# Decoder layer: attention scores take two pairs of PSUM banks in turn, probabilities get eight places, and the units are put in another order

## The reference

```
x = layernorm(x + self_attention(x))        # 16 heads; keys and values from a latent of 64, queries from one of 128
x = layernorm(x + cross_attention(x, ctx))  # 16 heads of 16; keys = values = ctx; out @ W.T + b
x = layernorm(x + experts(x))               # 8 experts of 256 -> 1024 -> 256, the best 2 of each token, weighted

scores = where(causal, q @ k.T / sqrt(48), -inf); out = softmax(scores) @ v     # self: content 16 + rotary 32 per head
h = gelu(x @ W1[e] + b1[e]);  y = h @ W2[e] + b2[e];  out = sum over the two experts e of weight * y
```

## Time and profile before

| | us |
|---|---|
| median of 3 runs | 747.67 (745.39 to 748.39) |
| the profiled execution | 746.01 |
| its span in the trace | 744.2 |
| TensorE busy | 623.2 (84%) |
| VectorE busy | 514.3 (69%) |
| ScalarE busy | 399.4 (54%) |
| GpSimd busy | 286.7 (39%) |

### The profile page before, as it was taken

How to read it: one execution, slowest core, us unless ns; L and a number is a source line. 1 busy time by engine, 2 the same in 40 slices (tenths; PEclk the granted TensorE clock), 3 DMA queues, 4 the chain that set the end, 5 groups by cost and what they waited for, 6 DMA issues and landing times.

```text
span 744.2 us, 22691 instructions
## 1 busy us (share of the span) xinstructions
PE 623.2 (84%) x8063; PEld 453.2 (61%) x8064; DVE 514.3 (69%) x1106; ACT 399.4 (54%) x847; POOL 286.7 (39%) x245
## 2 busy tenths in 40 slices
PE   3778889889999999888867677689999999999940
PEld 2456656666766666555644445667777777777720
DVE  6898789777866777546667764677766666666635
ACT  4345766667576574575865556344444444444414
POOL 3988454324555441511111010332444444454422
PEclk9899999999999999999997799799999999999985
DMA  8426551140403203213243014311222232222326
GB/s 274 118 65 172 160 165 37 46 142 11 106 3 100 59 13 121 70 37 80 77 152 89 27 57 142 114 31 30 45 44 45 45 52 42 42 42 42 49 41 208
DMA packets 39839, 59.45 MB, mean 80 GB/s; under 512 B 6768, under 2 KB 27504, under 8 KB 39632
## 3 DMA queue, kind: packets, MB, share of 16 engines
q1 hardware_dynamic: 32272, 48.12, 21.9%
q0 software_dynamic: 7488, 10.23, 8.5%
HBM read 34.08 MB, written 11.67 MB: 61 GB/s over the span
## 4 chain that ended last, share of the span: by engine, by line
PE 55%; issue 14%; DVE 13%; DMA 7%; ACT 6%; SPq 3%; POOL 1%; ACTq 1%; DVEq 0%; POOLq 0%
PE bank L1670 7%; PE bank L1272 4%; PE bank L1298 4%; PE bank L1672 4%; PE exp_scores L1323 3%; PE bank L1660 3%; DVE mxc L1062 3%; PE bank L1251 2%; PE max_scores L1660 2%; ACT probs L725 2%; PE bank L1662 2%; PE max_scores L1662 2%; PE max_scores L1661 2%; PE bank L1661 2%; PE bank L1252 2%
## 5 line engine op out<-in xcount | busy, mean ns | idle before, releaser
L725 ACT ACTIVATE probs<-exp_scores 128x768 f32<-128x768 f32 (+1 forms) x128 | 117.5, 918 | 118.5 <-PE exp_scores L1329 56.2
L615 POOL DMA_INDIRECT acc_rows<-x,slot_row x39 | 65.0, 1666 | 131.6 <-DVE x L1178 128.6
L1670 PE MATMUL bank<-w_sb,wp 128*128 x312 | 109.9, 380 | 1.6 <-DVE wp L1165 1.6
L1062 DVE TENSOR_REDUCE mxc<-max_scores 128x4 f32<-128x1024 f32 x64 | 78.1, 1221 | 38.2 <-PE max_scores L1343 38.0
L1672 PE MATMUL bank<-w_sb,wp 128*128 x312 | 85.0, 273 | 0.0
L794 ACT ACTIVATE probs<-bank,b_sb 128x128 f32<-128x128 f32 x152 | 43.5, 370 | 66.2 <-PE bank L1662 66.2
L794 ACT ACTIVATE probs<-max_scores,b_sb 128x128 f32<-128x128 f32 x160 | 45.6, 369 | 60.8 <-PE max_scores L1662 60.7
L1027 DVE TENSOR_REDUCE mx<-max_scores 128x6 f32<-128x768 f32 x64 | 61.0, 952 | 23.9 <-PE max_scores L1311 23.3
L1163 DVE CAST wp<-probs 128x512 f16<-128x512 f32 x78 | 33.8, 433 | 62.2 <-ACT probs L794 61.9
L1272 PE MATMUL bank<-probs,w_sb 128*32 128x256 f32 x768 | 57.3, 402 | 9.4 <-ACT probs L725 7.8
L1660 PE MATMUL max_scores<-xT,w_sb 128*128 128x128 f16 x320 | 61.3, 223 | 2.4 <-DVE xT L1157 2.4
(11 more groups left out here) (263 smaller groups left out, 1730.2 us busy)
## 6 DMA issues: line engine op xcount, KB each, us to landing
w_sb<-w_sb SPq DMA_DIRECT2D x192, 64.0 KB, 2.1
wstage<-in_w_exp SPq DMA_DIRECT2D x16, 512.0 KB, 4.2
w_sb<-in_w_exp SPq DMA_DIRECT2D x8, 512.0 KB, 4.9
wp<-in_w_exp SPq DMA_DIRECT2D x8, 512.0 KB, 3.8
x_sb<-in_x_by_feature SPq DMA_DIRECT2D x8, 256.0 KB, 3.6
x_res<-in_x SPq DMA_DIRECT2D x8, 256.0 KB, 3.0
ctx_raw<-in_ctx SPq DMA_DIRECT2D x8, 256.0 KB, 3.1
x_rows<-x SPq DMA_DIRECT2D x8, 256.0 KB, 2.7
```

The source lines that it names most:

```text
L615: nc.gpsimd.indirect_dma_start(out=acc_rows[:, :], out_offset=bass.IndirectOffsetOnAxis(ap=slot_row[:, n:n + 1], axis=0), in_=yb[n % 2], i ...
L725: nc.scalar.activation(probs[:, 2 * (k % 2):2 * (k % 2) + 2, 0:cols], ps_e[:, :, 0:cols], ACT.Exp, scale=(SELF_SCALE, CROSS_SCALE)[a]).the ...
L1062: nc.vector.tensor_reduce(mxc[:, 2 * k:2 * k + 2, :], ps_m[:, :, :].rearrange("p h (a k) -> p h a k", a=2), axis=AX.X, op=ALU.max).then_in ...
L1670: mm(o[:, 0:2 * D], ah[:, u, f, :], weights(e, at, 2 * D), start=(f == 0), stop=(f == FC - 1), skip_group_check=True)
```

## The change

- The two pairs of banks become `ps_p[0]` and `ps_p[1]`. A string of 288 digits, `SCORE_PAIRS`, says for each `sm`, `cm`, `st`, `se` and `ce` in TensorE's order which pair it takes; nearly always it is the other one than the unit before took (six times the same). `pair_free` waits for the reader of whatever unit was last in that pair. A stack now takes the first bank of its pair.
- `probs` gets eight places: groups of four heads alternate between two halves. The scratch that GpSimd's dynamic transfers use for their descriptors is halved (8192 bytes of each partition), as `probs` grows by 8192.
- All five orders are rewritten. Where TensorE's old order mostly alternated exponential units and maxima (94 exponential units stood alone between maxima or stacks), the new one has only 18 such and many runs of two to eight of one kind. `ge.4` moves from among the last `cm.7` to behind `cs.6` in VectorE's order, that is from before to after the maxima of batch 7 are complete. `gf.4` and `gR.4` move ahead of `cw.7`, and `gg.4` ahead of `cr.7` on GpSimd.
- New units `ft.4`, `fh.4`, `fl.4` transpose and split the slots of tile 0 inside attention, `ft.4` just before the last `lg.7` on TensorE, `fl.4` just before `lg.7` on VectorE.
- Several uses of the other banks move: `rope0` to bank 2, the gate's slots and table to bank 3, `cross_out` to bank 0, `cross_norm` to banks 0 and 1, and the two transposed maxima change places.
- The last tile: TensorE starts its first four `down` when the first half is split, and VectorE weights tile 37 before it splits the second half of tile 38.

The core of the diff:

```diff
+def pairs_in_turn():
+
+    uses = [x for x in order(TENSOR_ORDER) if x[0] in ("self_max", "cross_max", "stack", "self_exp", "cross_exp")]
+    return {use: int(bit) for use, bit in zip(uses, SCORE_PAIRS.replace("\n", ""))}
...
-        ps_fin = [ps_x[2], bank[1]]
+        ps_slots = [ps_x[3][:, 0:2 * P], bank[1][:, T:T + 2 * P]]
+        ps_fin = [ps_x[3], bank[1]]
         ps_kv, ps_q = ps_x[1], ps_x[1]
-        ps_qk = [ps_x[i] for i in (3, 1)]
-        ps_max = [ps_x[i] for i in (2, 0)]
+        ps_qk = [ps_x[i] for i in (2, 1)]
+        ps_max = [ps_x[i] for i in (0, 2)]
         ps_o = [[ps_x[i] for i in (0, 2)], [ps_x[i] for i in (1, 0)]]
-        ps_tok = [[ps_x[i] for i in (2, 0)], [ps_x[i] for i in (2, 1)]]
+        ps_tok = [[ps_x[i] for i in (2, 0)], [ps_x[i] for i in (0, 1)]]
         ps_back = [ps_x[i] for i in (0, 1)]
-        ps_out = [ps_x[i] for i in (0, 1)]
-        ps_sh = [ps_m[:, i, :].bitcast(F16) for i in range(2)]
+        ps_out = [ps_x[i] for i in (0, 0)]
+        ps_first = ps_x[1]
...
+                    half = k // 2 % 2
                     if k % 2 == 0:
                         for i in range(2):
-                            if done["exp", i] // 2:
-                                act_e.wait_ge(pe_pv[i], done["exp", i] // 2)
+                            if done[half, i]:
+                                act_e.wait_ge(pe_pv[i], done[half, i])
                     cols = (3 * P, 2 * T)[a]
-                    nc.scalar.activation(probs[:, 2 * (k % 2):2 * (k % 2) + 2, 0:cols], ps_e[:, :, 0:cols], ACT.Exp,
+                    nc.scalar.activation(probs[:, 2 * (k % 4):2 * (k % 4) + 2, 0:cols], ps_p[pair[u, k, b]][:, :, 0:cols], ACT.Exp,
                                          scale=(SELF_SCALE, CROSS_SCALE)[a]).then_inc(a_p[a], 1)
-                    done["exp", a] += 1
+                    if k % 2:
+                        done[half, a] = b * (H // 4) + k // 2 + 1
...
-            tile(N_TILES - 1, 0, False)
+            split_hidden(N_TILES - 1, 0, 0)
             weigh(N_TILES - 2, 1, (N_TILES - 3) * 16)
+            split_hidden(N_TILES - 1, 0, 1)
             weigh(N_TILES - 1, 0, (N_TILES - 2) * 16)
...
-            def exps_free():
-
-                once(a_p[0], at["self_exp"])
-                once(a_p[1], at["cross_exp"])
-
-            def maxima_free():
-
-                once(v_max[0], at["self_max"])
-                once(v_max[1], at["cross_max"])
+            held = [None, None]
+
+            def slots_in(n, u, loaded, target):
+
+                pe.wait_ge(g_ld[u], loaded)
+                for c in range(DC):
+                    last = nc.tensor.transpose(target[:, c * P:(c + 1) * P], xg[u][:, c * P:(c + 1) * P], ident)
+                last.then_inc(pe_ft, 1)
+
+            def pair_free(i):
+
+                if held[i]:
+                    once(*held[i])
...
                 elif u == "self_exp":
-                    exps_free()
+                    pair_free(pair[u, k, b])
...
                     last.then_inc(pe_t[0], 1)
-                    at[u] = b * (H // 2) + k + 1
+                    held[pair[u, k, b]] = a_p[0], b * (H // 2) + k + 1
                 elif u == "cross_exp":
-                    exps_free()
+                    pair_free(pair[u, k, b])
...
-            pe.wait_ge(v_al, 2 * N)
-            for f in range(FC):
-                down(0, f, last_at)
+            for half in range(2):
+                pe.wait_ge(v_al, 2 * N - 1 + half)
+                for f in range(4 * half, 4 * half + 4):
+                    down(0, f, last_at)
...
-    nc = bacc.Bacc("TRN2", target_bir_lowering=False, num_devices=1)
+    nc = bacc.Bacc("TRN2", target_bir_lowering=False, num_devices=1, dynamic_dma_scratch_size=8192)
```

The orders from batch 7's last maxima on, before and after. TensorE:

```diff
-cv1.6 st0.7 st1.7 ce5.6 x2.5 cm0.7 gr.4 cv2.6 ce6.6 cm1.7 lg.5 cm2.7 cm3.7 ce7.6 st2.7 st3.7 cm4.7 cv3.6 gs0.4 cm5.7
-co.6 cm6.7 cb.6 cm7.7 gs1.4 cn.7 ce0.7 cw.6 ce1.7 cv0.7 ce2.7 ce3.7 gs2.4 cv1.7 ce4.7 ce5.7 cv2.7 ce6.7 x2.6 ce7.7
-gs3.4 cv3.7 co.7 cb.7 gs4.4 cw.7 gf.4 lg.6 x2.7 lg.7
...
+ce4.6 ce5.6 cv1.6 ce6.6 ce7.6 st0.7 x2.5 st1.7 cm0.7 gr.4 st2.7 cv2.6 cv3.6 cm1.7 cm2.7 co.6 cm3.7 gs0.4 st3.7 cb.6
+cm4.7 lg.5 cm5.7 cm6.7 cm7.7 gs1.4 cw.6 cn.7 ce0.7 ce1.7 gs2.4 ce2.7 ce3.7 cv0.7 ce4.7 ce5.7 cv1.7 gs3.4 ce6.7 ce7.7
+cv2.7 cv3.7 x2.6 co.7 gs4.4 cb.7 gf.4 cw.7 lg.6 x2.7 ft.4 lg.7
```

ScalarE and VectorE, after:

```diff
+wh1.6 cv2.6 cv3.6 vc.7 gw0.4 st3.7 gw1.4 cb.6 wh2.6 gw2.4 ce0.7 ce1.7 ce2.7 ce3.7 gw3.4 cv0.7 cv1.7 ce4.7 ce5.7 ce6.7
+ce7.7 wh3.6 cv2.7 cv3.7 gw4.4 wh0.7 x2.6 cb.7 wh1.7 wh2.7 wh3.7 x2.7 fh.4
...
+g1.4 ss.7 g2.4 cm0.7 g3.4 gh0.4 cm1.7 co.6 cm2.7 cm3.7 gS0.4 gh1.4 cm4.7 cm5.7 lg.5 cm6.7 cm7.7 cn.7 gh2.4 gS1.4 cc.7
+cw.6 wl1.6 cl.6 gS2.4 gh3.4 cs.6 ge.4 wl2.6 gh4.4 gS3.4 wl3.6 co.7 wl0.7 gS4.4 gR.4 wl1.7 cw.7 cl.7 cs.7 lg.6 wl2.7
+wl3.7 fl.4 lg.7
```

ScalarE and VectorE, before:

```diff
-cv2.6 wh0.6 cv3.6 gw1.4 cb.6 wh1.6 ce0.7 ce1.7 gw2.4 ce2.7 ce3.7 cv0.7 wh2.6 wh3.6 ce4.7 ce5.7 gw3.4 ce6.7 x2.6 cv1.7
-ce7.7 cv2.7 wh0.7 cv3.7 gw4.4 wh1.7 cb.7 wh2.7 wh3.7 x2.7
...
-ss.7 g2.4 wl3.5 cm0.7 g3.4 cm1.7 cm2.7 cm3.7 gh0.4 ge.4 cm4.7 gS0.4 gh1.4 cm5.7 co.6 cm6.7 cm7.7 cn.7 cc.7 gh2.4 lg.5
-cw.6 wl0.6 wl1.6 cl.6 gS1.4 gS2.4 gh3.4 wl2.6 wl3.6 cs.6 gS3.4 gh4.4 co.7 wl0.7 wl1.7 gS4.4 cw.7 cl.7 gR.4 cs.7 lg.6
-wl2.7 wl3.7 lg.7
```

More of the change, by code:

```diff
@@ L343, in decoder_layer @@
         raw_masks = probs[:, :, :].rearrange("p a n -> p (a n)")[:, 0:M_ALL]
-        ps_e = stack.enter_context(nc.psum_tensor("exp_scores", [P, 2, 512], F32))
-        ps_m = stack.enter_context(nc.psum_tensor("max_scores", [P, 2, 512], F32))
+        ps_p = [stack.enter_context(nc.psum_tensor(f"scores{i}", [P, 2, 512], F32)) for i in range(2)]
         ps_x = [stack.enter_context(nc.psum_tensor(f"bank{i}", [P, 512], F32)) for i in range(4)]
-        bank = [ps_e[:, 0, :], ps_e[:, 1, :], ps_m[:, 0, :], ps_m[:, 1, :]] + [a[:, :] for a in ps_x]
+        bank = [ps_p[i][:, j, :] for i in range(2) for j in range(2)] + [a[:, :] for a in ps_x]
+        pair = pairs_in_turn()
         ps_kvT, ps_v = ps_x[1], ps_x[3]
@@ L1182, in tile @@
                 if following:
-                    low_slots(n + 1, 1 - u)
+                    low_slots(n + 1, 1 - u, bank[0])
                 split_hidden(n, u, 1)
@@ L1189, in _ @@
             dve.wait_ge(v_rows, 1)
-            low_slots(0, 0)
             gate_choose(*GATE[1])
-            low_slots(1, 1)
+            low_slots(1, 1, bank[0])
             dve.wait_ge(b2_ld, 16)
@@ L1300, in project_heads, with self_max_part @@
                 last.then_inc(pe_w[a], 1)
-            def self_max_part(h, part):
-                hp, rows, s = h // 2, slice(QK * (h % 2), QK * (h % 2) + QK), ps_m[:, h % 2, :]
+            def self_max_part(h, part, b):
+                hp, rows, s = h // 2, slice(QK * (h % 2), QK * (h % 2) + QK), ps_p[pair["self_max", h // 2, b]][:, h % 2, :]
                 q, key = qk16[rows, hp, 0, 0:T], qk16[rows, hp, 0, T:2 * T]
@@ L1503, in _ @@
                         for h in (2 * k, 2 * k + 1):
-                            last = self_max_part(h, part)
+                            last = self_max_part(h, part, b)
                     last.then_inc(pe_max[0], 1)
-                    at[u] = b * (H // 2) + k + 1
+                    held[pair[u, k, b]] = v_max[0], b * (H // 2) + k + 1
                 elif u == "self_negate":
-                    bank2_free()
+                    bank0_free()
                     transpose_max(0, b)
@@ L1527, in _ @@
                         for h in (2 * k, 2 * k + 1):
-                            last = cross_exp_part(h, part)
+                            last = cross_exp_part(h, part, b)
                     last.then_inc(pe_t[1], 1)
-                    at[u] = b * (H // 2) + k + 1
+                    held[pair[u, k, b]] = a_p[1], b * (H // 2) + k + 1
                 elif u == "self_pv":
@@ L1581, in _ @@
                 elif u == "stack":
-                    maxima_free()
-                    if at["stack"] > 1:
-                        once(a_xc, at["stack"] - 1)
+                    pair_free(pair[u, k, b])
                     pe.wait_ge(a_x1h, b + 1)
@@ L1603, in _ @@
                         for h in (2 * k, 2 * k + 1):
[L1604 removed]
+                            last = cross_max_part(h, t, b)
                     last.then_inc(pe_max[1], 1)
[L1606 removed]
+                    held[pair[u, k, b]] = v_max[1], b * (H // 2) + k + 1
                 elif u == "x2_transpose":
@@ L1640, in _ @@
             pe.wait_ge(v_rows, 1)
-            def slots_in(n, u, loaded):
-                pe.wait_ge(g_ld[u], loaded)
-                for c in range(DC):
-                    last = nc.tensor.transpose(bank[0][:, c * P:(c + 1) * P], xg[u][:, c * P:(c + 1) * P], ident)
-                last.then_inc(pe_ft, 1)
             w_bytes = w_sb[:, :].bitcast(mybir.dt.uint8)
```

255 lines of the change are left out of this document (132 added, 123 removed), and 3 rows, old and new, of the table UNITS.

## The result

The changed kernel takes **707.04 us** (median of 4 runs, 706.66 to 708.42) against 746.53 us beside it: ratio 0.9474, 95% interval 0.9444 to 0.9505. I had forecast 728.6 with a range from 716.0 to 746.5.

The account below looks back on a forecast made before the run. Expert tiles were taken as matmul-bound (238 us, fixed), attention as holding 87 us without a matmul. Terms -8.6 - 3.5 - 6.2 - 0.8 = -19.1 took 746.01 to 726.9; plus 1.66 for the median, 728.6 us; range 716 to 746.5.

Parts of the forecast that it names:

- Pairs and places: TensorE's waits up to 400 us for score banks and probabilities, 25.9 us: -8.6 us, ends +22 and -17.
- I credit a third: Share of those 25.9 us expected to go, since a reader late because its engine is busy stays late: -8.6 us.
- The tile choice: `ge.4` moved out of batch 7's cross maxima on VectorE, hidden during the exponentials: -3.5 us, between 0 and -6.2.
- Batch 7's exponentials: ScalarE's last eight passes fall from 17.9 to 11.7 us: -6.2 us, between 0 and -8.
- To the experts: From batch 7's exponentials to the experts: early gathers and tile 0's slot units gain 0.
- I price this pair at 0: Slot rows known sooner on TensorE against two gathers ahead of GpSimd's last inverse root: 0, between +3.8 and -3.8.
- So the three new units are worth 0: `ft.4`, `fh.4`, `fl.4` before the experts: 0, since tile 1's low slots end the 7.0 us chain behind the last logits.
- The last tile: Weighting of tile 37 put ahead of the second split on VectorE: -0.8 us, ends 0 and -0.8.
- The 4.59 us between them stay: Distance between the issues of the two last scatters unchanged, so all behind moves by -0.8 us.
- Scratch and banks: Half the scratch for GpSimd's transfers and the other four banks' moved uses: both 0.
- Only the ends gain: VectorE sets batches 0 to 6 and the 25.9 us reappear as other waits: 737.2 us, chance 0.14.
- Rival 3: Exponential units behind a maximum wait for VectorE, 0.38 us each, 58 times: slower, 760.3 us, chance 0.13.

Follow-up runs that it names:

- Experiment 1: Kernel before, old orders, with pairs strictly in turn, eight places and half the scratch: 753.13 us (1.0078); pairs in turn alone, four places, full scratch: 757.34 us (1.0124).
- experiment 2: Changed kernel with the pairs fixed by kind again, new orders kept but for four moved units, eight places kept: 864.2 us, 1.1588 of the kernel before.
- experiment 5: Changed kernel with the gate's tile choice (gh0.4 and ge.4) back among batch 7's cross maxima on VectorE: 710.2 us.
- experiment 4: Kernel before with half the DMA scratch and nothing else: 746.22 us (1.0012).
- experiment 3: Changed kernel with the digits strictly 0101..., without the six places where a pair is used twice running: 709.8 us (0.9496).
- 9: Changed kernel with the last tile as it was, both splits ahead of the weighting of tile 37: 709.06 us.
- 7: Changed kernel with the first gathers behind the last inverse root on GpSimd, as before: 711.81 us (0.9517).
- 6: Changed kernel with batch 7's cross exponentials using only the first four places: 711.9 us (0.9500).
- 8: Changed kernel without the three units for tile 0's slots ahead of the experts: 710.56 us (0.9488).

## Why the prediction was right, and where it was wrong

**Pairs and places (-8.6 forecast, -16.9 and -4.1 measured).** The term was mis-sized: it measured -21.0 us, below the 25.9 that I had called the most but beyond my far end of -17. The step that failed is "I credit a third", with its reason that a busy reader is late all the same. Of 24.7 us of waits, 17.8 went (72%). TensorE's time without a matmul fell from 58.9 to 44.6 us up to batch 7's self maxima and by 3.2 more up to `x1`, together 17.5; the other 3.5 are matmul time (326.1 to 323.4 us, and 8.6 to 7.7 in the short stage, which holds 54 matmuls at a clock of 0.74 before and 91 at 1.00 after). And the term was credited to the wrong thing: I wrote "only the waits move" and priced the structure, as if the orders only said where it acts. Experiment 1 has the structure at +5.9 us, experiment 2 the orders at +117; the whole first term is an effect of both together. The Trainium skill's observation that PSUM double-buffering "gave no further gain" (TensorE: Matmul & The Clock Gate, "HAM oscillation — how this bites in real kernels") would have the term at 0. For the old orders the runs agree with it in that nothing is gained (1.0078; pairs alone 1.0124); for the new ones they don't.

**The tile choice (-3.5; 2.6 by experiment 5).** Right in mechanism and near in size. The second step that failed is a term that I put at nothing without a reason: the clock of that stage. The earlier trace rows show 0.76 from 400 to 434 us, and I read that number, named it, and then priced no change of it. It went with 6.4 us of the 9.0 in the first profile, and with some 3 less in the second, where the same program had 0.89. Over the whole span the matmuls took 12.6 us less, a third of the gain, and no term of my sum had any of it.

**Batch 7's exponentials (-6.2; the passes 17.9 to 11.0, the stage -8.3).** The step held: I forecast 11.7 us for the eight passes. (The two gate units of 2.0 us reach to a pass at 450.88 us that the earlier trace rows leave out; the reading is right.) The rest of the stage, 1.4 us, goes with the clock (0.94 to 1.00, matmuls 22.01 to 19.27 us): experiment 4's kernel, with the old orders and a clock of 1.00 there, takes 28.0 instead of 29.6 us.

**To the experts (0; -1.2).** Two errors that nearly hide each other. "I price this pair at 0": the gathers ahead of the root are worth 2.4 us once TensorE waits for the tile. "So the three new units are worth 0": they are worth 1.6, because I looked at TensorE's tile 0 and forgot what is queued behind the waiting instruction on VectorE. With the units and without the early gather the logits are 2.4 us late, more than the units gain; the change needs both. The last logits came 471.18 - 433.39 = 37.8 us earlier, not 18.

**The last tile (-0.8; -0.3).** "The 4.59 us between them stay" failed: 4.77.

**Scratch and banks (0).** Right for the scratch (experiment 4). The other four banks' new uses weren't tried alone: the orders are written for them.

**The rivals.** Only the ends gain: refuted by the first stage. The weight splits don't set the experts' start: low slots follow the logits by 5.3 us. Rival 3 is refuted for this kernel (1.7 us of such waits, against the 10 that I had set as the mark) but its mirror image, a maximum or a stack behind an exponential, is a part of what happens to the structure alone.

The chance for faster was 0.76. The range's lower end, 716, added the bounds of four terms. Three of them were passed: -21.0 against -17, -9.0 against -6.2, and -8.3 against -8, of which 3.5, 6.4 and some 2.7 us are matmul time, and the clock was in none of the bounds. Part of this is luck of the profile, since the -9.0 would be -6.0 in a middle one. The kernel's time doesn't rest on it: the second profile, with 3 us more in that stage, has the same span (704.9).

## What to carry to other kernels

A buffer that is shared in turn and the order of the work that uses it are one change: price them together, and expect either alone to lose. When a stretch has a granted clock below 1, its matmuls are a term of their own, since closing gaps there can also shorten the matmuls (here 12.6 of 39.4 us). For a unit that is moved, list what stands behind its wait on every engine, not only on the one that the unit loads.

## What the runs showed of the hardware

The same program had a granted clock of 1.00 in one profile and 0.89 in another in the 30 us of batch 7's cross maxima, with 19.09 and 23.14 us of matmuls. In the five variants of the changed kernel that don't touch the stage, or only its digits, its length went with the clock: 29.2 us at 0.94 (experiment 3), 30.3 and 30.8 at 0.89 (9 and 7), 31.9 and 32.4 at 0.84 (6 and 8). TensorE's time without a matmul hardly differs between them, 7.8 to 8.9 us. What makes the clock fall in one run and not in another is open.

Idle time of TensorE can come with slower matmuls, but need not. Up to batch 7's self maxima, experiment 2 has 88.3 us more without a matmul than the changed kernel, and its matmuls take 46.2 us more (clock 0.88 against 0.98). Pairs alone (experiment 1) have 15.1 us more without a matmul than the kernel before, and their matmuls take 0.4 us more (0.97 against 0.98).
